# The causal mask moves from TensorE's score products to VectorE's maximum pass, with new order tables for the attention stage

## The chip, the cores and the metric

The kernel runs on one core of a Trainium2 chip. The core has five engines with an instruction queue each: TensorE (PE, matrix products into the banks of PSUM), VectorE (DVE), ScalarE (ACT), GpSimd (POOL) and SyncE (SP, which issues most DMAs). Sixteen DMA engines move data between HBM and SBUF. An engine runs its own queue in order; between engines only semaphores set the order. The metric is the device time of one execution, in microseconds (us).

## What the kernel computes

Two transformer-like layers on x, 4 sequences of 512 tokens, width 256, in fp32. Layer 0 is an attention pooling and a mixture of 32 experts. Layer 1 adds a conditioned product, and then runs causal attention with 16 heads of 16 and a mixture of 8 experts. Cut to the part that the change touches (the kernel treats 16 blocks of 256 tokens, called batches below, as its sequences; LB is 16 and T is 256 in it):

```python
h = layernorm(x, ln1_g, ln1_b)
q, k, v = split(h @ Wqkv)                    # 16 heads of 16
q, k = rope(q), rope(k)
scores = einsum('bqhd,bkhd->bhqk', q, k) / sqrt(16)
scores = where(tril, scores, -1e9)           # the causal mask
probs = softmax(scores)                      # exp(s - max s) / sum
x = x + (probs @ v) @ Wproj
h2 = layernorm(x, ln2_g, ln2_b)
top_inds = top_k(softmax(h2 @ Wgate), 2)     # two of 8 experts per token
...                                          # experts on gathered rows, added to x
```

## The kernel before

The program has three stages. Up to about 608 us layer 0 is computed. From there to about 1095 us the attention of layer 1 runs, and from 1139 us to the end its experts. All instructions that the change touches belong to the attention stage.

Attention works on 16 batches of 256 tokens. The 16 heads of a batch are taken in four groups of four. For one group the scores fill three banks of PSUM, called parts: part 0 and part 1 hold the later 128 queries of two heads each against all 256 keys (128x512), part 2 holds the first 128 queries of all four heads against the first 128 keys (128x512). A part passes through these steps:

- scores (PE, L1337 to L1346): a product of the bf16 triangle `causal` with `ident_b` writes the mask into the bank, and the product of KS and QS is added to it. For parts 0 and 1 the mask product has 256 columns, for part 2 it has 512.
- row_max (DVE, L1553): one reduction gives the negated maxima of a part, 2 or 4 numbers per row, into `smax`.
- exp (ACT, L1459): one exponential for each head, from the bank to PN in SBUF, with the negated maximum as bias. There are two slots of PN (NPN is 2), and the bank is free when its exponentials are done (semaphore s_pn).
- turn_p (PE, L1365, then ACT, L1467): PN is transposed, and copied to PT.
- values (PE, L1378 and L1380): the products with the values of the group.

Around these steps stand those of a whole batch, which belong to neighbouring batches at any moment. "combine" (DVE, L1561) adds four gathered expert results of layer 0 to X; they are gathered by POOL's indirect DMAs "got" (L1292). "matrix" is the conditioned product (DVE writes XC, L1567). "norm 0" and "norm 1" are the statistics of the two layer norms (DVE, L1519 to L1524), after which POOL takes the power -1/2 (L1273, tile rs), and "scale 0" and "scale 1" apply them (DVE, L1528, tiles xn and XN; XN has two buffers). "qk" is the product with Wqkv (PE, L1412), whose two rotary products DVE writes (L1593, tile rm) and POOL adds (L1301 and L1302). "split" (ACT and DVE, L1597) cuts q and k into high and low parts, and "stack" (SP, L1268) moves these to QS and KS by 16 DMAs of 128 KB for a batch. "proj" writes the residual XR (DVE, L1613), "base" adds it to X (POOL, L1305) and SP sends X to `out` (L1241). "normed" (SP, L1244) sends XN to a table in HBM; the semaphores xn2_out release its buffer. "gate" gives the routing logits, copied by DVE (L1617). The routing of a pair of batches, "route" and "place", is DVE work on small tiles (L187 to L312), and "entry" writes it to a table by POOL's indirect DMAs (L1314), eight for each pair. So every second round holds a placement and its eight entries. Layer 0's results are gathered three batches ahead, so that the last rounds have no "got".

The order of all this is written out by hand. There is one table for each engine (PE_ROUND, DVE_ROUND, ACT_ROUND, POOL_ROUND, SP_ROUND, from L1138). `rounds(table)` goes through its table once for each i from -4 to 19, and emits a step with offset o for batch i+o if that batch exists. One pass is called a round here. A step that waits on an engine holds up all the later steps of that engine's table.

PE's light steps (all but scores, turn_p and values) take turns on two banks in the order of its table (`light_bank`), and each of them waits until the one before it on its bank has been copied (`light_free`).

Of the kernel before, what the change touches and what calls it, by code (L numbers as in the profile page):

```python
# [61 lines left out]
def shape_constants():  # L62
# [35 lines left out]
def _build(nc, ctx, io, out):  # L98
# [1016 lines left out]
    s_attn_in = sem("attn_weights_in")  # L1115
    s_got0, s_ws_in = sems("results0_in", NGA * TB), sems("matrix_in", 2)
    s_begun = sem("values_begun_masks_ready")
# [21 lines left out]
        ("rank", -3), ("scores", -1, 3, 0), ("turn_p", -1, 2, 2), ("scores", -1, 3, 1), ("values", -1, 1),  # L1139
        ("norm_turn", 1), ("turn_p", -1, 2, 0), ("turn_p", -1, 2, 1), ("gate_turn", -2), ("scores", -1, 3, 2),  # L1140
        ("qk", 1, 0), ("qk", 1, 1), ("values", -1, 2), ("turn_p", -1, 3, 2), ("gate", -2), ("turn_p", -1, 3, 0),
        ("turn_p", -1, 3, 1), ("scores", 0, 0, 0), ("scores", 0, 0, 1), ("scores", 0, 0, 2), ("turn_qk", 1, 0),
        ("values", -1, 3), ("v", 1), ("outputs", -1, 0), ("scores", 0, 1, 0), ("turn_p", 0, 0, 2),
        ("outputs", -1, 1), ("scores", 0, 1, 1), ("turn_qk", 1, 1), ("scores", 0, 1, 2), ("turn_p", 0, 0, 0),
        ("out_turn", -1), ("turn_p", 0, 0, 1), ("scores", 0, 2, 0), ("x_turn", 2), ("proj", -1),
        ("scores", 0, 2, 1), ("matrix", 2), ("turn_p", 0, 1, 2), ("scores", 0, 2, 2), ("turn_p", 0, 1, 0),
        ("values", 0, 0), ("turn_p", 0, 1, 1))
# [299 lines left out]
    def act_attn(e):  # L1447
        wait_experts0(e)
        e.wait_ge(s_attn_in, N_ATTN_IN)
        for step, b, d in rounds(ACT_ROUND):  # L1450
            if step == "exp":
# [463 lines left out]
```

## Time and profile before

| what | us |
|---|---|
| median of three runs | 1525.74 |
| lowest and highest of them | 1524.75, 1528.5 |
| the profiled execution | 1527.01 |
| its span, first to last instruction | 1525.2 |
| busy: PE, DVE, ACT, POOL | 1392.3, 1033.8, 906.0, 721.4 |

The profiled execution lies 1.27 us above the median, and its span 1.81 us below its own time. The shares of busy time are means over three stages with different limits, so that the attention stage is read by itself: by stretches of one round each, by the timelines of its engines, and by the groups of instructions in it. In a timeline row the first number is the start in us, the second the duration, and a bracket at the end tells how long the engine had been idle and what released it. Durations of neighbouring instructions overlap in the pipeline, so the pace of a chain is read from one start to the next.

### The profile page before, as it was taken

How to read it: one execution, taken by the hardware profiler on the slowest of the kernel's cores; microseconds unless marked ns; L12 is line 12 of the kernel's file. 1: busy time of each engine (PE TensorE's matmuls, PEld its weight loads, DVE VectorE, ACT ScalarE, POOL GpSimd, SP SyncE). 2: the span in 40 equal slices, each digit the busy share in tenths (PEclk: the TensorE clock that was granted, in tenths of full speed). 3: DMA queues.
4: the chain of work that ended last, by engine and by line, in shares of the span. 5: the costliest groups of instructions: out<-in, count | busy, mean ns of one | idle time of the engine just before them, and what ended most of it. 6: DMA issues, size and time to landing. Idle time of an engine off the chain costs nothing.

```text
span 1525.2 us, 27526 instructions
## 1 busy us (share of the span) xinstructions
PE 1392.3 (91%) x9776; PEld 1221.8 (80%) x9776; DVE 1033.8 (68%) x2435; ACT 906.0 (59%) x2156; POOL 721.4 (47%) x720
## 2 busy tenths in 40 slices
PE   7997699999999999589999999999519999999996
PEld 5876599999999998358778777777419999998996
DVE  2999477777777775567888988895526556556552
ACT  5886255555555543158888888888526546456452
POOL 0788653444344204435465665653252435445333
PEclk9998899999999999689999999999859999999999
DMA  5421256566666614287868678686351343234212
GB/s 171 146 78 37 62 161 181 170 186 180 177 178 186 181 53 123 53 138 139 170 119 165 151 142 172 130 134 104 111 141 21 90 104 95 58 79 100 39 22 28
DMA packets 139449, 182.00 MB, mean 119 GB/s; under 512 B 22486, under 2 KB 107297, under 8 KB 139313
## 3 DMA queue, kind: packets, MB, share of 16 engines
q1 hardware_dynamic: 111152, 128.28, 33.6%
q0 software_dynamic: 28160, 51.96, 16.8%
q8 instruction: 79, 1.29, 0.4%
q14 instruction: 58, 0.47, 0.1%
HBM read 107.28 MB, written 42.08 MB: 98 GB/s over the span
## 4 chain that ended last, share of the span: by engine, by line
PE 78%; DVE 9%; issue 5%; POOL 3%; DMA 2%; ACT 2%; SPq 1%; POOLq 0%; DVEq 0%; ACTq 0%
PE banks L921 50%; PE banks L1365 5%; PE banks L1322 5%; PE banks L1412 3%; PE banks L440 3%; PE banks L983 2%; PE banks L1378 2%; PE banks L1339 2%; DVE lane_at L504 1%; PE banks L1759 1%; PE banks L1426 1%; DVE X L1561 1%; POOL table L1314 1%; PE banks L1346 1%; PE banks L1337 1%
## 5 line engine op out<-in xcount | busy, mean ns | idle before, releaser
L921 PE MATMUL banks<-hi_x,hi_w 128*128 128x320 f32 (+1 forms) x832 | 286.8, 345 | 10.7 <-DVE hidden L956 5.1
L921 PE MATMUL banks<-lo_x,hi_w 128*128 128x320 f32 (+1 forms) x832 | 285.6, 343 | 0.0
L921 PE MATMUL banks<-hi_x,lo_w 128*128 128x320 f32 (+1 forms) x832 | 285.2, 343 | 0.0
L921 PE MATMUL banks<-hi_w,hi_h 128*128 128x256 f32 x896 | 260.2, 290 | 2.1 <-DVE X L1010 1.7
L921 PE MATMUL banks<-lo_w,hi_h 128*128 128x256 f32 x896 | 253.5, 283 | 0.0
L921 PE MATMUL banks<-hi_w,lo_h 128*128 128x256 f32 x896 | 253.5, 283 | 0.0
L863 POOL DMA_INDIRECT xe<-pooled,idx x160 | 156.3, 977 | 198.6 <-PE banks L983 149.2
L1746 POOL DMA_INDIRECT out<-X,tab x64 | 106.5, 1664 | 204.7 <-DVE X L1843 190.1
L1459 ACT ACTIVATE PN<-banks,smax 128x256 f32<-128x256 f32 (+1 forms) x512 | 180.3, 443 | 15.9 <-DVE smax L1553 15.9
L921 PEld LDWEIGHTS banks<-hi_x,hi_w 128*128 128x128 f32 x832 | 158.3, 190 | 24.3 <-issue 10.4
L921 PEld LDWEIGHTS banks<-hi_w,hi_h 128*128 128x128 f32 x896 | 171.2, 191 | 3.3 <-issue 1.3
L921 PEld LDWEIGHTS banks<-lo_w,hi_h 128*128 128x128 f32 x896 | 171.5, 191 | 0.3
L921 PEld LDWEIGHTS banks<-hi_w,lo_h 128*128 128x128 f32 x896 | 171.3, 191 | 0.0
L921 PEld LDWEIGHTS banks<-hi_x,lo_w 128*128 128x128 f32 x832 | 158.0, 190 | 13.2
L921 PEld LDWEIGHTS banks<-lo_x,hi_w 128*128 128x128 f32 x832 | 158.3, 190 | 12.0
L1292 POOL DMA_INDIRECT got<-done,slot x128 | 124.5, 973 | 89.4 <-DMA done<-res 56.4
L1804 ACT ACTIVATE hidden<-banks,b1s 128x512 f32<-128x512 f32 x128 | 87.8, 686 | 122.8 <-PE banks L921 122.8
L1832 DVE TENSOR_TENSOR lo_h<-hidden,hi_h 128x512 fp32r<-128x512 f32 x128 | 88.3, 691 | 76.4 <-ACT hi_h L1809 76.4
L1553 DVE TENSOR_REDUCE smax<-banks 128x2 f32<-128x512 f32 (+1 forms) x192 | 126.8, 681 | 10.5 <-PE banks L1339 8.9
L956 DVE TENSOR_TENSOR hidden<-gate,banks 128x320 f32<-128x320 f32 (+1 forms) x144 | 73.4, 510 | 83.3 <-PE banks L921 74.9
L947 ACT ACTIVATE gate<-banks 128x320 f32<-128x320 f32 (+1 forms) x144 | 65.5, 455 | 97.6 <-PE banks L921 97.5
L1467 ACT ACTIVATE PT<-banks 128x512 f32<-128x512 f32 x192 | 114.5, 615 | 14.3 <-PE banks L1365 13.4
(186 smaller groups left out, 3051.4 us busy)
## 6 DMA issues: line engine op xcount, KB each, us to landing
w<-in_L_ffn_w SPq DMA_DIRECT2D x96, 256.0 KB, 5.8
done<-res SPq DMA_DIRECT2D x32, 640.0 KB, 3.9
QS<-parts_qk SPq DMA_DIRECT2D x128, 128.0 KB
KS<-parts_qk SPq DMA_DIRECT2D x128, 128.0 KB, 8.1
BIG<-in_L_ffn_W SPq DMA_DIRECT2D x16, 1024.0 KB, 9.6
mask<-in_c_masks SPq DMA_DIRECT2D x16, 257.0 KB, 2.8
pooled<-XF SPq DMA_DIRECT2D x16, 256.0 KB, 3.2
WS<-in_L_cond_W SPq DMA_DIRECT2D x16, 256.0 KB, 5.7
```

The costliest lines, as they stand in the source:

```text
L863: e.indirect_dma_start(xe[:, n % NXE, i, :], None, pooled, bass.IndirectOffsetOnAxis(ap=idx0[:, n * NS0 + i:n * NS0 + i + 1], axis=0)).the ...
L921: last = e.matmul(o, a[i], b[j], start=start and k == 0, stop=stop and k == 2, skip_group_check=True)
L956: e.tensor_tensor(hidden[:, i, 0:w], gate[:, i, 0:w], PS[:, up_bank(pt, unit) + 1, 0:w], ALU.mult).then_inc(s_hidden, 1)
L1292: e.indirect_dma_start(got0[:, b % NGA, t, k, :], None, done0, bass.IndirectOffsetOnAxis(ap=slot0[:, TB * b + t, k:k + 1], axis=0)).then_i ...
L1322: last = e.matmul(PS[:, bank, t * D:(t + 1) * D], src[:, c, t * P:(t + 1) * P], w(c), start=(c == 0), stop=(c == DC - 1))
L1365: last = e.transpose(PS[:, bank, k * P:(k + 1) * P], src, ident[:, :])
L1459: e.activation(PN[:, slot, part, x * width:(x + 1) * width], PS[:, part, x * width:(x + 1) * width], ACT.Exp, bias=smax[:, slot, col + x:c ...
L1467: e.activation(PT[:, G % NPN, part, :], PS[:, TBANK + n % 2, :], ACT.Copy).then_inc(s_pt, 1)
L1553: e.tensor_reduce(smax[:, G % NPN, col:col + heads_], PS[:, part, :].rearrange("p (x k) -> p x k", x=heads_), AX.X, ALU.max, negate=True). ...
L1746: e.indirect_dma_start(out_rows, bass.IndirectOffsetOnAxis(ap=who(u, i), axis=0), res1[:, u % 3, i, :], None, bounds_check=N - 1, oob_is_e ...
L1804: e.activation(hidden1[:, m % NHF, :], PS[:, 2 + m % 3, :], ACT.Gelu, bias=b1s[:, n, d:d + 1]).then_inc(s_hidden1, 1)
L1832: e.tensor_tensor(lo_h1[:, d, :], hidden1[:, m % NHF, :], hi_h1[:, d, :].bitcast(F32), ALU.subtract).then_inc(s_h1_lo, 1)
```

## The change

The mask products on PE are gone, with the tiles `causal` and `ident_b` and the two casts that made them. A tile `masks` (128 zeros, then the triangle) is loaded. The maximum pass becomes one fused instruction for each head: it adds the mask to the scores in the bank, writes the negated sum to PN, and gives its minimum, which is the negated maximum. The exponential then works in place in PN, with scale -1, and waits for each head. A bank of scores is now free when DVE has passed it (s_smax), and the wait for a free slot of PN is DVE's instead of ACT's. The small copy of the routing logits ("gate") moves from DVE to ACT. Two loads share another semaphore in the last stage.

```diff
-    tri_q = np.where(p[None, :] > p[:, None], -1e9, 0.0)
+    tri_q = np.concatenate([np.zeros((P, P)), np.where(p[None, :] > p[:, None], -1e9, 0.0)], 1)
...
 def pe_scores(e, G, part):
         if G >= 1:
-            e.wait_ge(s_pn, exp_count(G - 1, part))
-        if part < 2:
-            pair = 2 * g + part
-            e.matmul(PS[:, part, :].rearrange("p (h a k) -> p h a k", h=HQ, a=2)[:, :, 1, :], ident_b[:, :],
-                     wide(causal[:, :], 1, [P, HQ, P]), start=True, stop=False, skip_group_check=True)
...
+            e.wait_ge(s_smax, exp_count(G - 1, part))
+        for x in range(1 if part < 2 else 2):
+            pair = 2 * g + (part if part < 2 else x)
+            o, q, k = ((PS[:, part, :], QS[b % 2][:, pair, P:T], KS[b % 2][:, :, pair, :]) if part < 2 else
+                       (PS[:, 2, x * T:(x + 1) * T], QS[b % 2][:, pair, 0:P], KS[b % 2][:, :, pair, 0:P]))
+            last = e.matmul(o, q, k, start=True, stop=True, skip_group_check=True)
...
 def act_attn(e):
-                e.wait_ge(s_smax, 3 * G + part + 1)
-                if G >= NPN and part == 0:
-                    e.wait_ge(s_pt_ps, 3 * (G - NPN + 1))
                 for x in range(heads_):
-                    e.activation(PN[:, slot, part, x * width:(x + 1) * width], PS[:, part, x * width:(x + 1) * width], ACT.Exp,
-                                 bias=smax[:, slot, col + x:col + x + 1]).then_inc(s_pn, 1)
+                    s = PN[:, slot, part, x * width:(x + 1) * width]
+                    e.wait_ge(s_smax, 8 * G + col + x + 1)
+                    e.activation(s, s, ACT.Exp, bias=smax[:, slot, col + x:col + x + 1], scale=-1.0).then_inc(s_pn, 1)
...
 def dve_attn(e):
                 if G >= NPN and part == 0:
-                    e.wait_ge(s_pn, 8 * (G - NPN + 1))
-                e.tensor_reduce(smax[:, G % NPN, col:col + heads_], PS[:, part, :].rearrange("p (x k) -> p x k", x=heads_),
-                                AX.X, ALU.max, negate=True).then_inc(s_smax, 1)
+                    e.wait_ge(s_pt_ps, 3 * (G - NPN + 1))
+                for x in range(heads_):
+                    cols = slice(x * width, (x + 1) * width)
+                    e.tensor_tensor_reduce(PN[:, slot, part, cols], PS[:, part, cols], masks[:, T - width:], -1.0, 3.0e38,
+                                           ALU.add, ALU.min, smax[:, slot, col + x:col + x + 1]).then_inc(s_smax, 1)
...
     SP_ROUND = (
-        ("base", -3), ("weights", 2), ("stack", 1, 0), ("stack", 1, 1), ("normed", -2))
+        ("normed", -3), ("weights", 3), ("stack", 2, 0), ("stack", 2, 1), ("base", -1))
```

All five tables are new. Three places show what they move.

The first is DVE, where a pair of batches gets its slots (`slot`, step "place"), before the change: the placement stands behind the two scalings (XN and xn) and ahead of both sums of gathered results (X) and the rotary products (rm).

```order
L1528 TENSOR_SCALAR xn<-XC,mv,rs 128x256 [waits xn_turned,inverse_deviation0]
L1528 TENSOR_SCALAR xn<-XC,mv,rs 128x256
L294 TENSOR_TENSOR sm<-banks,small 128x32 [waits route1_ranked]
L295 TENSOR_REDUCE add<-sel 128x8
L297 SCALAR_TENSOR_TENSOR sm<-banks,sm 128x32 [waits dve_steps]
L299 TENSOR_TENSOR cum<-cum,add 128x8 [waits dve_steps]
L304 TENSOR_TENSOR pick<-hit,sm 128x64 [waits route1_placed]
L310 TENSOR_REDUCE sf<-pick 128x8 [waits route1_picked]
L312 TENSOR_SCALAR slot<-sf 128x8 [waits dve_steps]
L1561 SCALAR_TENSOR_TENSOR X<-got,w_pick,X 128x256 [waits results0_in2]
L1561 SCALAR_TENSOR_TENSOR X<-got,w_pick,X 128x256 [waits results0_added] x3
L1553 TENSOR_REDUCE smax<-banks 128x2 [waits exponentials,scores_part0]
```

After the change the same placement stands at the end, behind the second sum and ahead of the maxima of the next batch's first group (the fused pass is called ISA here).

```order
L1552 SCALAR_TENSOR_TENSOR X<-got,w_pick,X 128x256 [waits results0_in3]
L1552 SCALAR_TENSOR_TENSOR X<-got,w_pick,X 128x256 [waits results0_added] x3
L294 TENSOR_TENSOR sm<-banks,small 128x32 [waits route1_ranked]
L295 TENSOR_REDUCE add<-sel 128x8
L297 SCALAR_TENSOR_TENSOR sm<-banks,sm 128x32 [waits dve_steps]
L299 TENSOR_TENSOR cum<-cum,add 128x8 [waits dve_steps]
L304 TENSOR_TENSOR pick<-hit,sm 128x64 [waits route1_placed]
L310 TENSOR_REDUCE sf<-pick 128x8 [waits route1_picked]
L312 TENSOR_SCALAR slot<-sf 128x8 [waits dve_steps]
L1544 ISA PN,smax<-banks,masks 128x256 [waits weights1_turned,scores_part0]
```

Moved is "place": from a point behind "scale 0" to the last point ahead of the next batch's maxima.

The second is POOL in a round with entries, before: the four entries (`table`) that stand ahead of these rows go first, then the rotary sums (rm), and then the rest mixed with the gathers (got), the residual sum and the two powers (rs).

```order
L1302 TENSOR_TENSOR rm<-rm 128x8x32
L1301 TENSOR_TENSOR rm<-rm 128x8x32 [waits rotary_products]
L1302 TENSOR_TENSOR rm<-rm 128x8x32
L1314 DMA table<-pair,slot 8192x2 x2
L1292 DMA got<-done,slot 128x256 [waits results0_added]
L1292 DMA got<-done,slot 128x256 x3
L1314 DMA table<-pair,slot 8192x2 x2
L1292 DMA got<-done,slot 128x256 x2
L1305 TENSOR_TENSOR X<-X,XR 128x512 [waits residual_ready]
L1273 TENSOR_TENSOR rs<-ve,nhalf 128x2 [waits variance1]
L1292 DMA got<-done,slot 128x256
L1273 TENSOR_TENSOR rs<-ve,nhalf 128x2 [waits variance0]
```

After: rotary sums and residual sum come ahead, and all eight entries with six gathers stand between them and the power for "scale 0" (variance0).

```order
L1303 TENSOR_TENSOR X<-X,XR 128x512 [waits residual_ready]
L1312 DMA table<-pair,slot 8192x2 [waits route1_weighted,route1_slots]
L1312 DMA table<-pair,slot 8192x2
L1290 DMA got<-done,slot 128x256
L1312 DMA table<-pair,slot 8192x2 x2
L1290 DMA got<-done,slot 128x256
L1312 DMA table<-pair,slot 8192x2 x2
L1290 DMA got<-done,slot 128x256 x2
L1312 DMA table<-pair,slot 8192x2 x2
L1290 DMA got<-done,slot 128x256 x2
L1271 TENSOR_TENSOR rs<-ve,nhalf 128x2 [waits variance0]
L1290 DMA got<-done,slot 128x256 [waits results0_added]
```

The gathers and entries behind the rotary sums are now one block of 14, with the power at its end.

The third is SP's queue, around the stacking of one batch, before: the table transfer (normed) follows at once.

```order
L1268 DMA QS<-parts_qk 16x4x512 [waits scores_part2,qk_lo]
L1268 DMA QS<-parts_qk 16x4x512 x7
L1268 DMA KS<-parts_qk 16x4x512 [waits qk_lo]
L1268 DMA KS<-parts_qk 16x4x512 x7
L1244 DMA normed<-XN 128x2x256 [waits xn2_ready]
L1241 DMA out<-X 128x2x256 [waits base_ready]
L1251 TENSOR_LOAD in_itok_B_30_ptr [waits conditioned]
L1251 REGISTER_ALU
L1251 TENSOR_LOAD in_itok_B_30
L1251 ISA x2
```

After: the transfer of X to `out` follows first, and then "normed", whose batch is by one round older than before beside the same stack (offset -3 at the head of a round, behind a stack of offset 2 in the round ahead; it was -2 behind a stack of offset 1).

```order
L1266 DMA QS<-parts_qk 16x4x512 [waits scores_part2,qk_lo]
L1266 DMA QS<-parts_qk 16x4x512 x7
L1266 DMA KS<-parts_qk 16x4x512 [waits qk_lo]
L1266 DMA KS<-parts_qk 16x4x512 x7
L1239 DMA out<-X 128x2x256 [waits base_ready]
L1242 DMA normed<-XN 128x2x256 [waits xn2_ready]
L1249 TENSOR_LOAD in_itok_B_30_ptr [waits conditioned]
L1249 REGISTER_ALU
L1249 TENSOR_LOAD in_itok_B_30
L1249 ISA x2
```

Counted in batches, "normed" of batch b is now issued behind the stack of batch b+4; it stood behind the stack of batch b+3.

## Rows read from the trace of the kernel before

**Rows 1.** Windows, rounds: PE, PEld, DVE, ACT, POOL busy (x), clock, DMA share, GB/s.
```profile
714.54:741.22 26.68, 26.68 (x214) 20.96 (x213) 21.57 (x49) 22.73 (x64) 13.73 (x16) 1.00 0.80 154
767.90:795.00 27.10, 27.10 (x219) 21.33 (x220) 22.89 (x54) 22.02 (x59) 17.44 (x20) 1.00 0.79 150
795.00:822.37 27.37, 26.55 (x213) 20.63 (x211) 24.66 (x66) 23.70 (x65) 17.67 (x19) 1.00 0.74 154
960.00:987.33 27.33, 26.53 (x213) 20.60 (x211) 23.94 (x65) 23.65 (x65) 17.64 (x19) 1.00 0.85 155
1041.72:1070.31 28.59, 26.55 (x223) 22.06 (x223) 17.83 (x50) 25.79 (x75) 9.89 (x10) 0.94 0.71 112
```

**Rows 2.** Timeline, PE (start, us, engine, line, operation): mask product, score, transposes.
```profile
797.89 0.27 PE L1337 MATMUL banks<-causal,ident_b 128*128 128x256 bf16 x1
...
798.24 0.60 PE L1365 MATMUL banks<-ident,PN 128*128 128x128 f32 x4
...
799.89 0.38 PE L1342 MATMUL banks<-causal,ident_b 128*128 128x512 bf16 x1
...
800.34 0.60 PE L1365 MATMUL banks<-ident,PN 128*128 128x128 f32 x4
```

**Rows 3.** Timeline, DVE: three maxima in a row; the top-8 choice; layer norm; rotary products.
```profile
794.45 1.87 DVE L1553 TENSOR_REDUCE smax<-banks 128x2 f32<-128x512 f32 x3
...
796.94 0.77 DVE L234 MAX8 tv<-ex 128x8 f32<-128x8 f32 x4
...
801.93 0.08 DVE L238 MATCH_VALUE_LOAD ti<-tv,ex 128x8 f32 x1
...
803.66 0.68 DVE L1553 TENSOR_REDUCE smax<-banks 128x2 f32<-128x512 f32 x1
...
807.43 0.75 DVE L1519 BATCH_NORM_STATS2 st<-XC 128x6 f32<-128x256 f32 x2
...
808.57 0.69 DVE L1553 TENSOR_REDUCE smax<-banks 128x4 f32<-128x512 f32 x1
...
815.15 1.29 DVE L1593 TENSOR_TENSOR rm<-banks,ropec 128x512 f32<-128x512 f32 x2 [1.45 <-PE banks L1412]
```

**Rows 4.** Timeline, DVE: the fused mask and maximum in layer 0's pooling.
```profile
40.61 0.42 DVE L695 CUSTOM_DVE_ANT_0 pr<-banks,mask 128x256 f32<-128x256 f32 x1 [0.44 <-PE banks L585]
...
40.96 0.42 DVE L695 CUSTOM_DVE_ANT_0 pr<-banks,mask 128x256 f32<-128x256 f32 x1
```

**Rows 5.** Timeline, POOL, the same stretch.
```profile
40.32 0.72 POOL L272 TENSOR_TENSOR two<-hit 128x256 f32<-128x256 f32 x1 [39.35 <-DVE hit L246]
```

**Rows 6.** Lines by form, ACT: exponential from PSUM, exponential from SBUF.
```profile
L1459 ACT ACTIVATE PN<-banks,smax 128x256 f32<-128x256 f32 x225 | 93.8, 493 | 0.1
L643 ACT ACTIVATE pr<-pr,nmax 128x256 f32<-128x256 f32 x32 | 16.0, 503 | 3.9 <-DVE nmax L695 3.8
```

**Rows 7.** Timeline, POOL: scatters and gathers of attention.
```profile
785.94 1.00 POOL L1314 DMA_INDIRECT table<-pair,slot  x1 [0.30 <-issue]
...
796.35 0.97 POOL L1292 DMA_INDIRECT got<-done,slot  x1 [0.30 <-issue]
...
806.87 0.72 POOL L1273 TENSOR_TENSOR rs<-ve,nhalf 128x2 f32<-128x2 f32 x1 [0.56 <-DVE ve L1524]
...
839.07 1.01 POOL L1314 DMA_INDIRECT table<-pair,slot  x1 [1.61 <-DVE slot L312]
```

**Rows 8.** Timeline, DVE: slots of a pair, and sums of gathered results.
```profile
838.10 0.17 DVE L312 TENSOR_SCALAR slot<-sf 128x8 uint32<-128x8 f32 x1
838.18 2.04 DVE L1561 SCALAR_TENSOR_TENSOR X<-got,w_pick,X 128x256 f32<-128x256 f32 x4
...
844.95 3.72 DVE L1561 SCALAR_TENSOR_TENSOR X<-got,w_pick,X 128x256 f32<-128x256 f32 x4
```

**Rows 9.** Timeline, SP: stacking of one batch and what follows it.
```profile
797.05 5.19 SPq L1268 DMA_DIRECT2D QS<-parts_qk  x8
...
807.87 0.59 SPq L1244 DMA_DIRECT2D normed<-XN  x1
808.51 0.51 SPq L1241 DMA_DIRECT2D out<-X  x1
```

**Rows 10.** Tile XN: its transfer to the table in HBM.
```profile
DMA to landing us min/median/max: 2.2/8.7/12.2
```

**Rows 11.** Timeline, PE, end of attention: the longest wait of its transposes.
```profile
1059.39 0.66 PE L1365 MATMUL banks<-ident,PN 128*128 128x128 f32 x4 [1.41 <-ACT PN L1459]
```

More of the change, by code:

```diff
@@ L1138, in _build @@
     PE_ROUND = (
[L1139 to L1147, printed above, removed]
-    DVE_ROUND = (
-        ("route", -3, 3), ("row_max", -1, 2, 0), ("proj", -2), ("row_max", -1, 2, 1), ("norm", -2, 1),
-        ("matrix", 1), ("norm", 1, 0), ("row_max", -1, 2, 2), ("scale", -2, 1), ("scale", 1, 0), ("place", -3),
-        ("combine", 2, 0), ("row_max", -1, 3, 0), ("row_max", -1, 3, 1), ("qk", 1, 0), ("row_max", -1, 3, 2),
-        ("qk", 1, 1), ("combine", 2, 1), ("gate", -2), ("route_shift", -2), ("row_max", 0, 0, 0),
-        ("row_max", 0, 0, 1), ("row_max", 0, 0, 2), ("split", 1, 0), ("route", -2, 1), ("outputs", -1, 0),
-        ("row_max", 0, 1, 0), ("outputs", -1, 1), ("row_max", 0, 1, 1), ("split", 1, 1), ("row_max", 0, 1, 2),
-        ("route", -2, 2))
@@ new lines, in _build @@
+        ("scores", 0, 1, 2), ("out_turn", -1), ("turn_p", 0, 0, 0), ("scores", 0, 2, 0), ("turn_p", 0, 0, 1),
+        ("scores", 0, 2, 1), ("x_turn", 2), ("proj", -1), ("scores", 0, 2, 2), ("matrix", 2),
+        ("turn_p", 0, 1, 2), ("scores", 0, 3, 0), ("turn_p", 0, 1, 0))
+    DVE_ROUND = (
+        ("route_shift", -3), ("outputs", -2, 0), ("outputs", -2, 1), ("row_max", -1, 1, 0),
+        ("row_max", -1, 1, 1), ("split", 0, 1), ("row_max", -1, 1, 2), ("route", -3, 1), ("route", -3, 2),
+        ("row_max", -1, 2, 0), ("proj", -2), ("row_max", -1, 2, 1), ("row_max", -1, 2, 2), ("matrix", 1),
+        ("norm", 1, 0), ("row_max", -1, 3, 0), ("row_max", -1, 3, 1), ("scale", 1, 0), ("norm", -2, 1),
+        ("route", -3, 3), ("combine", 2, 0), ("row_max", -1, 3, 2), ("qk", 1, 0), ("scale", -2, 1), ("qk", 1, 1),
+        ("combine", 2, 1), ("place", -3), ("row_max", 0, 0, 0), ("row_max", 0, 0, 1), ("split", 1, 0),
+        ("row_max", 0, 0, 2))
@@ L1327, in pe_scores @@
         b, g = divmod(G, NG)
-        if G == 0 and part == 0:
-            e.wait_ge(s_begun, 4)
         if part == 0 and g == 0:
@@ L1511, in act_attn @@
                                  bias=lng[:, 3, c:c + 1], scale=lng[:, 2, c:c + 1]).then_inc(s_h2T, 1)
+            elif step == "gate":
+                half = (b % GB) * TB * E1
+                e.wait_ge(s_lg1, b + 1)
+                e.activation(lgs[:, half:half + TB * E1], PS[:, light_bank["gate", b, d], 0:TB * E1], ACT.Copy).then_inc(s_lgs, 1)
             elif step == "route_exp" and pair_begins(b):
```

67 lines of the change are left out of this document (28 added, 39 removed).

## Prediction

> **What bounds the kernel now.** I read the attention stage by itself, first the windows of one round each. In a round without placements PE is busy for all of its 26.68 us, while DVE has 21.57, ACT 22.73 and POOL 13.73 [rows 1]. The eight rounds from 767.90 to 987.33 hold placements, entries and gathers; a pair of them takes (987.33 - 767.90) / 4 = 54.86 us. There PE is still busy for 26.5 to 27.1 of about 27.4 us, DVE for 22.9 to 24.7, and POOL's load has risen to 17.5. The reader is to see that PE is the bound and that DVE is the next one, 3 to 4 us behind it. Second, the timelines: how long each instruction keeps its engine is the distance to the next start, as the printed durations overlap. Third, the queues that DVE depends on (POOL and SP), since a new order can make these late although they are not busy for the whole round.
>
> **PE.** A mask product and its score take 798.24 - 797.89 = 0.35 us for 256 + 512 columns, and for part 2, with 512 + 512 columns, 800.34 - 799.89 = 0.45 [rows 2]. By columns the mask is 0.11 of the first and 0.22 of the second. A batch has 8 of the first and 4 of the second: 8 x 0.11 + 4 x 0.22 = 1.76 us. PE's round falls from 26.68 to 24.9, and over 16 batches 28 us is the most that the change can give.
>
> **DVE.** Twelve reductions go; three in a row take 1.87 of which the last is 0.68, so that one costs 0.60 [rows 3]: 7.2 us per batch. In come 32 fused passes, 16 of 128x256 and 16 of 128x128. The wide one runs in layer 0, at 40.96 - 40.61 = 0.35 (its accumulator read included) [rows 4]. The narrow one is in no row. It costs no less than half of the wide one, 0.17, and no more than the wide one, 0.35. From 0.60 for 512 columns and 0.35 for 256, 128 columns come to 0.22, and I take this. So 16 x 0.345 + 16 x 0.22 = 9.0 (bounds 8.2 and 11.1), which is 1.8 more than before. The gate copy takes 0.1 off every round. DVE's pair of rounds, 22.89 + 24.66 = 47.55, becomes 51.0, which is 25.5 a round: DVE overtakes PE. In the rounds without routing it has 21.57 + 1.8 = 23.4, under PE.
>
> The Trainium skill ("VectorE: DVE Perf Modes", section on the TRN2 errata) charges a VectorE instruction reading PSUM 120 cycles and one per column at 0.96 GHz. That would be 0.39 us for 256 columns and 0.26 for 128, an estimate of 10.4 us per batch instead of 9.0. It speaks against cutting one wide pass into heads; the pace of 0.35 in the trace is below its 0.39 [rows 4], so that I stay with the rows. By the page the sum below would hardly move, because the waits below absorb slower passes, but the first rival would lose most of its gain.
>
> **ACT.** The exponentials read SBUF instead of PSUM: 503 ns in layer 0 against 493 [rows 6], 0.3 for 32; the gate copy adds 0.2. From 22.0 to 23.7 ACT rises to at most 24.2, still behind DVE and PE. This costs nothing as long as these are later.
>
> **Wait 1, POOL.** The power for "scale 0" now stands behind a block of eight entries and six gathers, and the block can't start before "place", which has moved to the end of DVE's round. An entry costs 1.00 + 0.30 and a gather 0.97 + 0.30 [rows 7]: 8 x 1.30 + 6 x 1.27 = 18.0 us. The first entry starts 839.07 - 838.27 = 0.8 after the end of the slots [rows 7, 8]. With 0.72 for the power the scaling can go on 19.5 us after the slots. What DVE has to do between: 16 wide passes 5.5; 12 narrow ones 2.6; two splits, XR and XC, each at the 0.60 of a 512-wide pass, 2.4; two scalings of outputs 1.4 (an estimate from 0.35 a pass and as much for the reciprocal); the choice of experts, 0.77 for MAX8 and 803.66 - 801.93 = 1.73, 2.5; one norm 808.57 - 807.43 = 1.14 [rows 3]. The sum is 15.5. So DVE stands still for 4.0 us in each round after a placement (bounds 2.5 and 5). Behind "scale 0" on DVE are the sums, the rotary products and the maxima of the last group; PE's qk and then everything of the next batch waits for these. Before, POOL had the same entries, but "place" came a round's half earlier, and its powers were ready for DVE's statistics: the power at 806.87 waited for DVE [rows 7].
>
> **Wait 2, SP.** "normed" of a batch b-2 now goes out behind the stack of batch b+2 and one transfer to `out`, and "scale 1" of batch b must wait until it has landed, because XN has two buffers. From the start of QS to the issue of "normed" 807.87 - 797.05 = 10.8; the transfer to `out` ahead of it 808.51 - 807.87 = 0.64; its own issue 0.59; then the landing, median 8.7 [rows 9, 10]. That is 20.7 us after the first split. DVE's work from there to "scale 1": 12 wide passes 4.1, 16 narrow 3.5, split, XR and XC 1.8, two norms 2.3, outputs 1.4, "scale 0" 0.7, the first sum 2.0, rotary products 1.3, and some 0.7 of waiting for PE's qk (it is 1.45 before [rows 3], and more work lies ahead of it now): 17.8. The stall is 3.0, with the landings from 2.2 to 12.2 anything from none to 6. In the round with wait 1 it is hidden by that; so it is due once in a pair. Before, this transfer had a round more.
>
> **The sum.** A pair: 51.0 of work, 4.0 and 3.0 of the waits, twice 0.7 for qk: 59.4 against 54.86, which is +4.5, and for four such pairs +18. Three early rounds without routing and without a second use of XN run at PE's new pace, 3 x -1.8 = -5.4. The last three rounds have no gathers, so that the block of POOL is short; there PE and DVE share the limit and I take -1.3 each, -4. The clock: after an idle time of 1.41 us PE was granted a lower clock in the stage's end, 0.94 in the mean of that round [rows 1, 11]. In rounds with stalls PE has 4 us to spare, so that I take only +2 for all (bounds 0 and 14). Start and end of the stage I count as unchanged, within 1 us. Together +10.6: 1527.0 + 10.6 = 1537.6 for an execution like the profiled one, and less the 1.3 that this lies above the median, 1536. This case has its own range from 1524 (landings early, entries 1.2 us faster) to 1550.
>
> **Rivals.**
> 1. Neither wait decides, because DVE comes later to "scale 0" and "scale 1" than my sums say, or POOL's block runs faster. Then the eight rounds take DVE's 25.5 instead of 27.4, -15.4, and with the 9.4 of the other rounds the time is 1501. For it speaks that the pure work of every engine fits into 25.5 us, and that only 2 to 4 us of slack are missing; against it that POOL's pace is the same in each row. It decides if the slots are done 4 us earlier than I put them.
> 2. One of the waits decides, the other doesn't. With wait 1 alone a pair is 56.4 (+1.5), with wait 2 alone 55.4 (+0.5): 4 x +1 - 9.4 = -5, 1520. For it speaks that the landing varies from 2.2 to 12.2 [rows 10].
> 3. Each stall lowers PE's clock, and PE's products at 1.2 GHz then lie on the chain to DVE: some 1.5 us for each of eight stalls, 1550. Before, one idle time of 1.41 did this [rows 11]; against it, PE has scores to run in most of a stall.
> 4. DVE's fused passes are held up by POOL as the sums are: four of these took 2.04 us at 838.18 and 3.72 at 844.95 [rows 8], where POOL was adding. By that ratio, for the two thirds of a round that POOL works, the passes would take 9.0 x 0.55 = 4.9 us more in a round: about 1600. Against it, in layer 0 the pace was 0.35 while POOL was at a product of 0.72 from 40.32 on [rows 4, 5].
>
> On the last, the Trainium skill ("SBUF — State Buffer", section "Who interferes with whom") says that a VectorE instruction with two inputs in SBUF contends with a GpSimd instruction that reads SBUF, and one with at most one such input does not. The sums have two and the fused pass one, so it agrees with both rows; by the page's rule rival 4 would be out altogether.
>
> **Chances.** My forecast 0.54; rival 1 0.17; rival 2 0.14; rival 3 0.08; rival 4 0.04; something else 0.03. A measurement of this kernel can tell about 0.3%, 4.6 us, from no change. Slower by more comes from most of my own case (0.42 of 0.54) and rivals 3 and 4: 0.55. Faster by more from rival 1, half of rival 2 and a little of the rest: 0.27. Within it 0.18. The range from 1500 to 1556 takes in rivals 1 and 2 and most of 3.
>
> **What would show it.** In the changed profile PE should have no bf16 products of 256 or 512 columns, and rounds without routing should last about 25 us. A wait of DVE's xn on POOL's rs of about 4 us in every second round, and one of DVE's XN on the transfer "normed" of about 3 us in the other, would show the two waits; PE's busy time in these rounds would fall to some 25 of 29 us. The fused narrow pass at a pace of 0.22 would show DVE's term. I am wrong if xn and XN hardly wait, or if rounds from 770 us on last 26 us or less.

## The result, and the profile after

The changed kernel took 1571.83 us (median of 4 runs, 1568.62 to 1577.71), the kernel before 1526.82 on the same chip: a ratio of 1.030, 95% interval 1.026 to 1.034. It is slower, by 45 us; forecast were 1536 and a range from 1500 to 1556. The direction was right, and the time lies outside the range. The profiled execution of the changed kernel has a span of 1566.9 us, 41.7 more than before.

The windows of rounds of the changed kernel, in the columns of [rows 1], cut where xn starts:

```profile
703.20:730.00 26.80, 25.67 (x202) 19.78 (x201) 24.52 (x101) 23.49 (x59) 14.27 (x16) 1.00 0.79 132
730.00:757.30 27.30, 26.17 (x203) 20.05 (x202) 25.97 (x112) 24.71 (x68) 14.07 (x16) 1.00 0.79 155
757.30:784.00 26.70, 25.39 (x200) 19.44 (x200) 24.91 (x103) 23.17 (x58) 14.16 (x16) 1.00 0.71 148
784.00:817.70 33.70, 27.95 (x215) 21.16 (x213) 27.75 (x121) 26.52 (x71) 21.85 (x23) 1.00 0.73 141
817.70:845.40 27.70, 25.71 (x191) 19.17 (x192) 24.97 (x101) 21.52 (x54) 14.42 (x16) 0.94 0.63 115
784.00:1033.60 249.60, 217.97 (x1621) 166.35 (x1620) 208.53 (x881) 192.49 (x497) 144.46 (x152) 0.95 0.69 131
1064.10:1092.00 27.90, 26.91 (x222) 20.39 (x220) 20.01 (x103) 26.07 (x66) 6.88 (x8) 1.00 0.69 100
```

The kernel before, its eight rounds for the same batches, cut at xn too ([rows 1] has them cut at another point):

```profile
782.02:1001.45 219.43, 214.67 (x1718) 167.91 (x1717) 190.93 (x473) 183.14 (x490) 141.10 (x153) 1.00 0.77 149
```

Three things can be read. A round without a placement takes 26.7 to 27.3 us ahead of the eight, as before, although PE is busy for only 25.4 to 26.2 of it. The first round that has a placement, up to the next xn, takes 33.7; the three others take 35.3, 37.0 and 34.7. And the eight rounds with placements, entries and gathers take 249.60 us, 62.4 for a pair, where they took 219.43 and 54.86: these alone are 30.2 us of the 41.7. Of the rest, 2.0 us had been lost when they begin (784.0 against 782.0), and 9.5 us are lost behind them. PE's granted clock in the eight is 0.95 in the mean, where it was 1.00.

What VectorE waited for from 650 to 1140 us in the changed kernel (waiting instruction, what released it; us in total, times, longest):

```profile
DVE XN L1518 <- issue: 16.6, 5, 6.4
DVE xn L1518 <- POOL rs L1271: 15.0, 4, 4.5
DVE XR L1603 <- PE banks L1320: 13.8, 10, 5.8
DVE rm L1584 <- PE banks L1400: 13.1, 14, 2.0
```

The first two are the two waits of the prediction. "issue" behind XN means that the profile shows no releaser; the next rows tell what it was. The queue of SP in the round that leads to one such wait, changed kernel:

```profile
843.59 0.58 SPq L1239 DMA_DIRECT2D out<-X  x1
844.22 0.50 SPq L1242 DMA_DIRECT2D normed<-XN  x1
```

"normed" is issued at 844.22, and XN, which needs that buffer, starts 10.5 us after that, at 854.71. In the trace the transfer lands at 854.62, 0.09 us before XN starts. VectorE in the same pair of rounds:

```profile
854.71 0.74 DVE L1518 TENSOR_SCALAR XN<-XR,mv,rs 128x256 f32<-128x256 f32 x2 [2.60 <-issue]
...
856.56 3.63 DVE L1552 SCALAR_TENSOR_TENSOR X<-got,w_pick,X 128x256 f32<-128x256 f32 x4
...
861.06 0.17 DVE L312 TENSOR_SCALAR slot<-sf 128x8 uint32<-128x8 f32 x1
...
880.70 0.79 DVE L1518 TENSOR_SCALAR xn<-XC,mv,rs 128x256 f32<-128x256 f32 x2 [2.88 <-POOL rs L1271]
...
887.21 1.13 DVE L1518 TENSOR_SCALAR XN<-XR,mv,rs 128x256 f32<-128x256 f32 x2
```

XN has waited 2.60 us at 854.71, and xn 2.88 us at 880.70, for POOL. The latter's releaser, on POOL's timeline:

```profile
862.04 1.01 POOL L1312 DMA_INDIRECT table<-pair,slot  x1 [2.13 <-DVE slot L312]
863.35 1.00 POOL L1312 DMA_INDIRECT table<-pair,slot  x1 [0.30 <-issue]
864.65 0.99 POOL L1290 DMA_INDIRECT got<-done,slot  x1 [0.30 <-issue]
...
878.93 0.98 POOL L1290 DMA_INDIRECT got<-done,slot  x1 [0.30 <-issue]
879.92 0.75 POOL L1271 TENSOR_TENSOR rs<-ve,nhalf 128x2 f32<-128x2 f32 x1
```

The slots are done at 861.23, the first entry starts 0.8 later, as in [rows 7], and the power ends at 880.67, which is 19.4 us behind the slots. The prediction had 19.5.

Last, the end of the stage, where the prediction had seen no wait; one of XN on VectorE, again for a transfer "normed" that had been issued at 1088.12:

```profile
1096.69 0.74 DVE L1518 TENSOR_SCALAR XN<-XR,mv,rs 128x256 f32<-128x256 f32 x2 [6.44 <-issue]
```

### The profile page after: what moved, and what is told of

Same layout as the page of the kernel before. It is cut to its first block, busy times and chain, and to the rows that moved or that the text cites. A ratio compares the mean times of both kernels' runs of the same rounds, so it can differ in the third digit from the quotient of the medians.

```text
span 1566.9 us, 27911 instructions
## 1 busy us (share of the span) xinstructions
PE 1395.2 (89%) x9584; PEld 1217.6 (78%) x9584; DVE 1066.6 (68%) x3249; ACT 923.9 (59%) x2172; POOL 727.3 (46%) x720
## 4 chain that ended last, share of the span: by engine, by line
PE 61%; DVE 12%; issue 7%; SPq 7%; DMA 6%; POOL 5%; ACT 2%; POOLq 0%; DVEq 0%; ACTq 0%
PE banks L921 49%; SPq L1266 5%; DMA normed<-XN 4%; DVE X L1552 2%; PE banks L983 2%; POOL table L1312 2%; DVE rm L1584 2%; PE banks L1353 1%; PE banks L1400 1%; PE banks L440 1%; PE banks L1320 1%; DVE PN L1544 1%; POOL got L1290 1%; DVE XN L1518 1%; PE banks L1745 1%
## 5 line engine op out<-in xcount | busy, mean ns | idle before, releaser
L1446 ACT ACTIVATE PN<-PN,smax 128x256 f32<-128x256 f32 (+1 forms) x512 | 191.4, 452 | 4.2 <-DVE smax L1544 3.3
L1544 DVE CUSTOM_DVE_ANT_0 PN<-banks,masks 128x256 f32<-128x256 f32 (+1 forms) x512 | 150.6, 351 | 11.9 <-PE banks L1335 6.2
L1353 PE MATMUL banks<-ident,PN 128*128 128x128 f32 x768 | 120.4, 285 | 7.3 <-ACT PN L1446 4.1
L1453 ACT ACTIVATE PT<-banks 128x512 f32<-128x512 f32 x192 | 110.9, 594 | 26.8 <-PE banks L1353 25.8
```

What stands on the lines that cost most here:

```text
L1353: last = e.transpose(PS[:, bank, k * P:(k + 1) * P], src, ident[:, :])
L1446: e.activation(s, s, ACT.Exp, bias=smax[:, slot, col + x:col + x + 1], scale=-1.0).then_inc(s_pn, 1)
L1453: e.activation(PT[:, G % NPN, part, :], PS[:, TBANK + n % 2, :], ACT.Copy).then_inc(s_pt, 1)
L1544: e.tensor_tensor_reduce(PN[:, slot, part, cols], PS[:, part, cols], masks[:, T - width:], -1.0, 3.0e38, ALU.add, ALU.min, smax[:, slot, c ...
```

## The experiments

Every run was compared with runs of the kernel before on the same chip. The runs fell on four chips, and on two of them the kernel before took 1662 and 1678 us instead of 1527. There engines stood idle for stretches that no instruction of the program ended, as in this row of VectorE's waits with the old tables (run e4_old_tables):

```profile
DVE rsum L1590 <- remote: 57.6, 11, 8.3
```

What these stretches are stays open. Times are compared on one chip only, between chips the ratios.

**e1_normed_early.** SP's transfer one batch earlier.

```diff
     SP_ROUND = (
-        ("normed", -3), ("weights", 3), ("stack", 2, 0), ("stack", 2, 1), ("base", -1))
+        ("normed", -2), ("weights", 3), ("stack", 2, 0), ("stack", 2, 1), ("base", -1))
```

> SP's table has the transfer normed one batch earlier (offset -2), so that it stands behind the stack of batch b+3 again; nothing else differs from the changed kernel. Theory W (the two queue waits and VectorE's own work add up on VectorE's chain): the waits of XN (12 us in the four pairs of rounds) go, the waits of xn on POOL stay, and the time falls by 10 to 16 us, from 1572 to 1556 to 1562. Rival F (the waits only fill time that VectorE would lose anyway to TensorE): XN's waits go and others take their place, time 1567 to 1573.

Measured: 1704.73 us against 1661.96 of before, ratio 1.026 (1.020 to 1.032). No wait of XN for its transfer is left. The chip was one of the slower two, where the changed kernel itself was not run, and xn's waits on POOL were down to 1.7 us in all. So this run by itself decides nothing.

**e2_power_early.** POOL's power behind two gathers instead of six.

```diff
     POOL_ROUND = (
-        ("got", 3, 0, 0), ("norm", -2, 1), ("got", 3, 0, 1), ("qk", 1, 0), ("qk", 1, 1), ("base", -2),
-        ("entry", -3, 0), ("got", 3, 0, 2), ("entry", -3, 1), ("got", 3, 0, 3), ("entry", -3, 2),
-        ("got", 3, 1, 0), ("got", 3, 1, 1), ("entry", -3, 3), ("got", 3, 1, 2), ("got", 3, 1, 3), ("norm", 2, 0))
+        ("got", 3, 0, 0), ("got", 3, 0, 1), ("got", 3, 0, 2), ("norm", -2, 1), ("got", 3, 0, 3), ("qk", 1, 0),
+        ("qk", 1, 1), ("base", -2), ("entry", -3, 0), ("entry", -3, 1), ("got", 3, 1, 0), ("entry", -3, 2),
+        ("got", 3, 1, 1), ("entry", -3, 3), ("norm", 2, 0), ("got", 3, 1, 2), ("got", 3, 1, 3))
```

> POOL's table has the power for scale 0 behind eight entries and two gathers instead of behind eight entries and six; four gathers follow it. SP's table as in the changed kernel. Theory W: xn's waits on POOL (15 us in four rounds) go, but part of each is then taken by the wait of XN on the transfer normed, which starts from an earlier point and was hidden in that round: time down by 8 to 15 us, to 1557 to 1564. Rival F: 1567 to 1573.

Measured on the same chip: 1687.07 us, ratio 1.017 (1.010 to 1.023), 17.7 less than with the other edit alone. One wait of XN of 6.3 us was left.

**e3_both and e8_both_again.** Both edits; first beside e1 and e2, then beside the changed kernel on one chip, which is run **e7_after_again**.

> Both edits. Theory W: no wait of over 1 us of xn or XN is left, a pair of rounds falls from 62.4 to about 55.5, and the time by 24 to 32 us, to 1540 to 1548. It stays slower than the kernel before, since VectorE's own work (some 26.5 us in a round) has taken TensorE's place as the bound. Rival F: 1560 to 1573. Rival P (VectorE has slack, and without the waits TensorE's shorter round shows): a pair at 50 to 51, time 1520 or less.

Measured: 1682.08 us, ratio 1.012 (1.006 to 1.017). It is 22.7 below e1 and 5.0 below e2. In e1's profile xn waits for POOL for only 1.7 us, so on this chip that wait doesn't account for the 22.7; what does is open. The two waits are therefore judged by the next pair of runs, on a quicker chip.

> The changed kernel as it is, as the reference of the next three on one chip. Ratio to the kernel before 1.03 again, if the loss doesn't depend on the chip; on a chip where rounds are longer for other reasons the waits of xn and XN could be smaller, ratio down to 1.02.

> Both order edits (normed one batch earlier, power for scale 0 behind two gathers instead of six), beside the changed kernel on one chip. Theory W: 24 to 32 us less than the changed kernel. Rival F (the waits only fill time that is lost anyway): 0 to 8 us less.

Measured: the changed kernel 1576.09 (ratio 1.031, 1.029 to 1.033), both edits 1543.90 (ratio 1.011, 1.009 to 1.014). That is 32.2 us less, where theory W had 24 to 32 and rival F 0 to 8. The waits removed had been 16.6 + 15.0 = 31.6 us in the first profile of the changed kernel. In that of e7, on the chip of e8, they are longer:

```profile
DVE XN L1518 <- issue: 20.7, 6, 6.4
DVE xn L1518 <- POOL rs L1271: 16.2, 4, 4.5
```

These are 36.9 us, and the profiled executions of e7 and e8 differ by 37.1. So the two waits cost about what they last, and F falls. The absolute time expected for both edits, 1540 to 1548, holds on this chip.

**e4_old_tables and e10_old_tables_again.** The new mechanism with the five tables of the kernel before; the logits copy is VectorE's again, since these tables have it there.

```diff
     SP_ROUND = (
-        ("normed", -3), ("weights", 3), ("stack", 2, 0), ("stack", 2, 1), ("base", -1))
+        ("base", -3), ("weights", 2), ("stack", 1, 0), ("stack", 1, 1), ("normed", -2))
...
```

> The mask on VectorE and the exponentials in place, with all five order tables of the kernel before and the logits copy on VectorE. Theory W (the new order causes the two waits, the mechanism only makes VectorE the bound): no waits of over 1 us on rs and normed, rounds of 26.5 to 27.5, time 1520 to 1535, about that of the kernel before. Rival M (the fused passes themselves, more passes in line with the same other work, cost the time): 1550 or more. Rival P: TensorE's 1.8 us a round shows, 1500 to 1510.

> The mask on VectorE with all five order tables of the kernel before, again; the first time the chip was one on which the kernel before took 1662 us. If the order makes the whole loss: ratio to the kernel before 0.99 to 1.005. If that first equality came from the chip's longer rounds, which hid a loss of VectorE's: 1.01 to 1.02.

Measured: 1661.60, ratio 1.000 (0.997 to 1.003), and on the quicker chip 1530.40, ratio 1.002 (1.000 to 1.004). So the mechanism alone, with 1.7 us more of VectorE in each of the eight rounds (204.62 us against 190.93) and its shorter TensorE, changes the time by no more than 0.4%, and the loss of the changed kernel comes with the new order. Rivals M and P both fall. The new tables were not run with the old mechanism, so it stays open whether they would cost as much without the move of the mask. The windows of e10 (two rounds without entries, then the eight with):

```profile
702.10:728.60 26.50, 25.03 (x196) 19.32 (x196) 23.46 (x100) 22.97 (x57) 13.47 (x16) 1.00 0.78 131
728.60:756.20 27.60, 25.93 (x212) 19.62 (x204) 25.30 (x118) 24.80 (x69) 13.61 (x16) 1.00 0.85 154
782.30:1005.30 223.00, 205.51 (x1628) 156.71 (x1624) 204.62 (x890) 190.00 (x489) 139.47 (x153) 1.00 0.76 148
```

PE is busy for 25.0 to 25.9 us in the first two, and for 205.51 of 223.00 in the eight; what PE saves it now spends waiting. PE's largest waits in the eight rounds:

```profile
PE banks L440 <- DVE xn L1514: 6.4, 8, 1.7
PE banks L1414 <- DVE parts_qk L1584: 5.9, 8, 1.1
```

**e5_base_later.** Both edits, and POOL's residual sum behind one gather.

```diff
-        ("got", 3, 0, 0), ("got", 3, 0, 1), ("got", 3, 0, 2), ("norm", -2, 1), ("got", 3, 0, 3), ("qk", 1, 0),
-        ("qk", 1, 1), ("base", -2), ("entry", -3, 0), ("entry", -3, 1), ("got", 3, 1, 0), ("entry", -3, 2),
+        ("got", 3, 0, 0), ("got", 3, 0, 1), ("got", 3, 0, 2), ("norm", -2, 1), ("qk", 1, 0), ("qk", 1, 1),
+        ("got", 3, 0, 3), ("base", -2), ("entry", -3, 0), ("entry", -3, 1), ("got", 3, 1, 0), ("entry", -3, 2),
```

> As the kernel with both edits, and POOL's residual sum (base) comes one gather later, so that it no longer runs beside the second sum of gathered results on VectorE. Theory W with VectorE as the bound: the second sum falls from 3.65 to about 2.7 us, and the time by 0.9 x 14 = 10 to 14 us against both edits. If VectorE isn't the bound: within 3 us of it.

Measured: 1546.59, against 1543.90 with both edits: nothing gained, a miss of theory W's 10 to 14. The sums became shorter by 7% only (625 ns each instead of 674), and their waits for gathered results longer (4.9 us instead of 2.7).

**e6_half_sums.** Both edits, with two of the four sums cut to 8 columns.

```diff
-                    e.scalar_tensor_tensor(X[:, tt, :], got0[:, b % NGA, d[0], k, :], w_pick0[:, tt, k:k + 1], X[:, tt, :],
+                    n = D if k < 2 else 8
+                    e.scalar_tensor_tensor(X[:, tt, 0:n], got0[:, b % NGA, d[0], k, 0:n], w_pick0[:, tt, k:k + 1], X[:, tt, 0:n],
                                            ALU.mult, ALU.add).then_inc(s_comb, 1)
```

> As the kernel with both edits, with a part of layer 1's input left out: of the four gathered results per token the third and fourth are added in 8 of 256 columns only, which takes about 2.4 us of VectorE's work out of each round. Theory W with VectorE as the bound: rounds without waits fall from 26.8 to TensorE's 25.5 to 26, the time by 15 to 30 us against both edits. If TensorE or a chain through all engines is the bound already: 0 to 6 us.

Measured: 1529.62, 14.3 less than both edits, just under theory W's 15 to 30. Less work was taken away than meant. The groups of the sums from 690 to 1040 (line, engine, operation, form, count; busy us, mean ns), first e8, then e6:

```profile
L1552 DVE SCALAR_TENSOR_TENSOR X<-got,w_pick,X 128x256 f32<-128x256 f32 x96 | 64.7, 674 | 5.2 <-DMA got<-done,slot 2.7
```

```profile
L1553 DVE SCALAR_TENSOR_TENSOR X<-got,w_pick,X 128x256 f32<-128x256 f32 x48 | 28.4, 592 | 6.6 <-DMA got<-done,slot 5.8
L1553 DVE SCALAR_TENSOR_TENSOR X<-got,w_pick,X 128x8 f32<-128x8 f32 x48 | 22.4, 468 | 1.7
```

64.7 us became 28.4 + 22.4 = 50.8, 13.9 us less. In the whole stage 81.5 became 36.8 + 26.9 = 63.7, 17.8 less, and the time fell by 14.3. So with the two waits gone most of VectorE's work counts. That it counts everywhere isn't shown: from the fourth xn to the last the two profiled executions differ by only 7.2 us (341.93 and 334.68), with 13.9 less of sums.

**e9_split_first.** In the profile of e8 one more wait shows, PE's, from 690 to 1040:

```profile
PE banks L1414 <- DVE parts_qk L1588: 17.2, 12, 2.0
```

This is the turning of the outputs (L1414). It uses the bank that holds q and k until VectorE has made the low part (parts_qk, step "split"). In e8's round at 854 that stood behind the second sum, the placement and four fused passes, first VectorE's rows, then PE's:

```profile
847.73 3.63 DVE L1552 SCALAR_TENSOR_TENSOR X<-got,w_pick,X 128x256 f32<-128x256 f32 x4
...
852.23 0.17 DVE L312 TENSOR_SCALAR slot<-sf 128x8 uint32<-128x8 f32 x1
...
854.09 0.69 DVE L1588 TENSOR_TENSOR parts_qk<-banks,parts_qk 128x512 fp32r<-128x512 f32 x1
```

```profile
854.83 0.66 PE L1414 MATMUL banks<-ident,oT 128*128 128x128 f32 x4 [2.03 <-DVE parts_qk L1588]
```

```diff
-        ("row_max", 0, 0, 0), ("row_max", 0, 0, 1), ("split", 1, 0),
+        ("split", 1, 0), ("row_max", 0, 0, 0), ("row_max", 0, 0, 1),
         ("row_max", 0, 0, 2))
```

> As the kernel with both order edits, and on VectorE the split of q's parts (split 1,0) stands ahead of the next batch's maxima of parts 0 and 1 instead of behind them. Theory S (a third wait: TensorE's turning of the outputs stands behind the shared bank that this split releases, 17 us in 12 waits from 690 to 1040, and it lies on the chain): the waits fall to under 0.6 us each and the time by 8 to 17 us against both edits, ratio to the kernel before 1.000 to 1.006. Rival D (VectorE's own work is the bound and the wait of TensorE costs nothing): 0 to 4 us, ratio 1.009 to 1.012.

Measured: 1537.53 against 1526.46 of before on its chip, ratio 1.006 (1.004 to 1.008). Over the kernel before it is 11.1 us where both edits had 16.6. The gain of 5.5 us by the medians, 8 by the ratios, is at or below the lower edge of theory S, and the ratio is outside what rival D had. What is left of the waits from 690 to 1040, on PE and on VectorE:

```profile
PE banks L1414 <- DVE parts_qk L1588: 5.2, 9, 1.1
```

```profile
DVE X L1552 <- DMA got<-done,slot: 8.5, 4, 3.4
```

The longest is 1.1 us, where under 0.6 was expected. The wait for gathers was 2.7 us in e8. It comes from the edit of POOL's table: the gathers stand behind the power, and arrive too late for the second sum.

**e12_no_new_waits and e13_old_tables_tuned.** e12 goes on from e9, with a new table for POOL and one step moved on VectorE:

```diff
     POOL_ROUND = (
+        ("got", 3, 0, 0), ("norm", -2, 1), ("got", 3, 0, 1), ("got", 3, 0, 2), ("qk", 1, 0), ("qk", 1, 1), ("base", -2),
+        ("got", 3, 0, 3), ("entry", -3, 0), ("got", 3, 1, 0), ("entry", -3, 1), ("got", 3, 1, 1), ("entry", -3, 2),
+        ("got", 3, 1, 2), ("got", 3, 1, 3), ("norm", 2, 0), ("entry", -3, 3))
...
-        ("row_max", -1, 3, 2), ("qk", 1, 0), ("scale", -2, 1), ("qk", 1, 1)
+        ("scale", -2, 1), ("row_max", -1, 3, 2), ("qk", 1, 0), ("qk", 1, 1)
```

e13 goes on from e10, with two exchanges on VectorE and one on POOL:

```diff
-        ("row_max", 0, 0, 2), ("split", 1, 0)
+        ("split", 1, 0), ("row_max", 0, 0, 2)
-        ("scale", -2, 1), ("scale", 1, 0)
+        ("scale", 1, 0), ("scale", -2, 1)
-        ("norm", -1, 1), ("got", 3, 1, 2), ("norm", 2, 0))
+        ("norm", -1, 1), ("norm", 2, 0), ("got", 3, 1, 2))
```

> As the kernel with both order edits and the split first, with POOL's table drawn up again: all gathers of a round stand ahead of the power for scale 0 and the last two entries behind it (with the gathers behind it, the second sum on VectorE waited 8.5 us for them in four rounds), and XN is scaled ahead of the rotary products, where POOL adds nothing (0.65 instead of 1.2 to 1.3 us). If what is left of the loss is the order's: the waits for gathers go, 6 to 14 us less than with the split first, ratio to the kernel before 0.997 to 1.002. If it is the mechanism's own work on VectorE: 0 to 4 us less, ratio 1.003 to 1.006.

> The mask on VectorE with the tables of the kernel before, and three exchanges in them: the split of q's parts ahead of the maxima of part 2, scale 0 ahead of scale 1, POOL's power for scale 0 ahead of a gather. TensorE waited 0.7 us for the split and 0.8 us for xn in each of eight rounds with the old tables. If these waits are on the chain, 8 to 16 us less than the old tables alone, ratio to the kernel before 0.992 to 0.997, faster than both kernels. If other engines' work follows at once: 0 to 4 us less, ratio 1.000 to 1.003.

Measured, on the slowest of the chips: e12 1679.53, ratio 1.002 (0.999 to 1.004), the kernel before 1677.58. In the profile of e12 VectorE's wait for gathers is gone. From 1.031 the new tables have come to 1.002 by order alone, with the mechanism untouched. The interval of e12 also takes in the lower part of what was expected if the mechanism's own work were left (1.003 to 1.006), so a small rest of that kind isn't excluded. e13 1683.95, ratio 1.004 (1.002 to 1.007), outside both of its expectations: its exchanges gained nothing, and no version beat the kernel before. Whether e12 or e13 would gain on a chip without the idle stretches wasn't tried.

## Why the prediction was wrong in size

**The two waits: right.** Each had its place, its releaser and about its size. POOL's was forecast at 4 x 4.0 us and came to 15.0 in four. SP's was forecast at 4 x 3.0: in the eight rounds it came three times, with 9.0 in all, a fourth time just behind them with 1.2, and with 6.4 more in the last rounds. Undoing both took 32 us away. PE's lower clock in these rounds came too; what it cost was not measured apart from the waits.

**The step that failed first: "Three early rounds ... run at PE's new pace, 3 x -1.8 = -5.4".** They gained nothing: from xn to xn the three take 80.83 us, where they took 80.02. PE's new pace was not what set them.
- PE's saving. PE's busy time fell from 26.68 to 25.7 (mean of the three rounds above), by 0.9, and with the old tables (e10) by 1.1 in the mean of the eight rounds (214.67 and 205.51, divided by 8). Forecast were 1.76. The price of one mask product was right where products follow each other without a wait. Four transposes and a wide score, with the mask, in the kernel before:

```profile
798.67 0.60 PE L1426 MATMUL banks<-ident,oT 128*128 128x128 f32 x4
799.11 0.27 PE L1337 MATMUL banks<-causal,ident_b 128*128 128x256 bf16 x1
799.14 0.48 PE L1339 MATMUL banks<-KS,QS 128*128 128x512 f32 x1
799.46 0.60 PE L440 MATMUL banks<-ident,rm 128*128 128x128 f32 x4
```

These take 799.46 - 798.67 = 0.79 us, and without the mask 745.91 - 745.24 = 0.67 (rows of the changed kernel below): 0.12 less, where the prediction had 0.11. Where the rest of the 1.76 went is open.
- DVE's work. The prediction took the lightest window, 21.57, for all early rounds. Every second round there has the choice of experts too, so that the mean of the three is 22.4 (67.13 / 3), and in the changed kernel it is 25.1 (75.43 / 3). Of the 8.3 us that this is more in three rounds, counted from each start to the next, the fused passes in place of the reductions make 4.4, the sums 2.8 and XN 1.3. So the passes cost 1.5 more in a round, where 1.8 was forecast; sums and XN, put at no change, cost another 1.3. With the pauses under 0.2 us between its instructions, 2.2 in all, DVE fills 77.6 of the 80.8 us, which leaves no room for the 24.9 us of PE's new pace. With the old tables (e10) DVE fills 73.9 of 80.2 us, and the three rounds are no shorter; what holds them there is open. The paces of the fused passes are 0.35 and 0.21, as forecast (first two rows 128x256, then 128x128):

```profile
728.60 0.42 DVE L1544 CUSTOM_DVE_ANT_0 PN<-banks,masks 128x256 f32<-128x256 f32 x1
...
728.95 0.42 DVE L1544 CUSTOM_DVE_ANT_0 PN<-banks,masks 128x256 f32<-128x256 f32 x1
...
733.87 0.28 DVE L1544 CUSTOM_DVE_ANT_0 PN<-banks,masks 128x128 f32<-128x128 f32 x1
...
734.08 0.28 DVE L1544 CUSTOM_DVE_ANT_0 PN<-banks,masks 128x128 f32<-128x128 f32 x1
```

The estimates of 0.39 and 0.26 from the Trainium skill ("VectorE: DVE Perf Modes", section on the TRN2 errata) are too long as paces by these rows.
- A wait that was missed. PE's outputs stand behind VectorE's split, through a shared bank. The changed kernel, PE in an early round:

```profile
742.62 0.96 PE L1429 MATMUL banks<-wgate,h2T 128*128 128x8 f32 x8
744.51 0.66 PE L1414 MATMUL banks<-ident,oT 128*128 128x128 f32 x4 [0.93 <-DVE parts_qk L1588]
744.92 0.48 PE L1335 MATMUL banks<-KS,QS 128*128 128x512 f32 x1
745.24 0.60 PE L1414 MATMUL banks<-ident,oT 128*128 128x128 f32 x4
745.59 0.48 PE L1335 MATMUL banks<-KS,QS 128*128 128x512 f32 x1
745.91 0.60 PE L1353 MATMUL banks<-ident,PN 128*128 128x128 f32 x4
```

PE is idle for 0.93 us at 744.51, and by the split of e8 for up to 2.03. The prediction wrote that in rounds with stalls "PE has 4 us to spare"; it asked what stands behind xn and XN, but not which of PE's steps stands behind a bank that VectorE has yet to leave. By the gain of e9 this wait lay on the chain in part of the stage. It did not hold up the early rounds: in e9 PE doesn't wait there for the split, and the three take 81.23 us.

**The second: the work of a pair, 51.0.** With the old tables (e10) it is right: 204.62 / 4 = 51.2. With the new ones DVE was busy for 208.53 / 4 = 52.1 us of a pair. To that come pauses between instructions that depend on each other, which the busy time of a window leaves out: 1.6 us of a pair, summed from those under 0.2 us. A sum of DVE's that is set against a round has to hold them. The waits came to 8.7 us of a pair, where 8.4 was forecast. The 1.1 us more of work lie in the sums and in XN, which now run beside POOL's adds. The first sum of a round takes 2.04 us, as before. The second takes 3.62 to 3.66 us in every round from 700 to 1044, where it took 2.4 to 2.7 and 3.6 to 3.8 in turn; the 3.72 of [rows 8] is one of the long ones. XN's scaling is told at the end. So what rival 4 had for the fused passes, that POOL holds them up, held for the sums and the scaling instead. By the ratios of e8, e9 and e12 most of the rest of the loss was order as well.

**The third: "The last three rounds have no gathers ... -4".** They gained nothing, and from the end of the eight rounds to the end of the program 9.5 us were lost. The wait of XN at 1096.69 took 6.44 us of it: without gathers and entries, VectorE comes to XN sooner, but "normed" is issued no sooner. The prediction looked for SP's wait only where POOL's was.

In sum: the eight rounds cost 30.2 us instead of 18, and the rounds ahead of them and behind them, forecast at -9.4, cost 2.0 and 9.5. The range was too narrow because its upper end had the waits at their longest, but every gain at its full size.

**Rivals.** 1 and 2 (a wait that doesn't decide) fell. 3 (PE's clock) can't be told apart from the waits. In the eight rounds PE was busy for 12.5 us longer than with the old tables at a clock of 1.00 (217.97 and 205.51), for nearly as many products; how much of that lay on the chain is open. With both edits (e8) the mean clock of these rounds is still 0.96. 4 fell: in e10, 75 of the fused passes overlap one of POOL's adds, and take 418 and 284 ns like the rest. That the mechanism alone would come to 1.002 was forecast by none of the prediction's cases: even with no new wait it gains nothing.

## What to carry to other kernels

When work moves from the engine that is the bound to the one behind it, the gain ends where that one becomes the bound: add up its work from start to start, pauses included, before counting the first engine's saving. A new order is priced queue by queue: for each wait, take the time from its releaser's start back to what that one waits for, and set it against the work of the engine that waits; this gave the mean of both waits over the four pairs to within 1 us (3.8 and 2.3 for 4.0 and 3.0), though not each one. Do the same for buffers and banks that two steps share, as these carry waits that no data shows.

## What the runs showed of the hardware that was not expected

A scaling pass on VectorE (TENSOR_SCALAR, one tensor from SBUF, 128x256) slows down when POOL adds in SBUF at the same time. In the changed kernel and with the old tables (e10), from 690 to 1040:

```profile
L1518 DVE TENSOR_SCALAR XN<-XR,mv,rs 128x256 f32<-128x256 f32 x22 | 11.9, 581 | 9.0 <-issue 9.0
```

```profile
L1514 DVE TENSOR_SCALAR XN<-XR,mv,rs 128x256 f32<-128x256 f32 x26 | 9.5, 408 | 0.0
```

In the first, XN stands between the two rotary products, whose sums POOL makes at that moment; in the second it stands ahead of them, and took 408 ns. Within the changed kernel the overlap decides: 21 of the 32 passes that write XN overlap one of POOL's adds and take 675 ns in the mean, the other 11 take 400 to 412. The same holds for the sums, which read two tensors from SBUF: 57 of 128 overlap an add and take 857 ns in the mean, the others 473 to 486. One of POOL's adds beside the pair of XN at 887.21 (1.13 us, above):

```profile
887.38 0.82 POOL L1299 TENSOR_TENSOR rm<-rm 128x256 f32<-128x256 f32 x1 [2.73 <-DVE rm L1584]
```

The Trainium skill ("SBUF — State Buffer", section "Who interferes with whom") counts tensor_scalar among the operations that can take the port pair shared with GpSimd, and the trace agrees, with 581 against 408 ns. The fused pass, with its one input in SBUF, kept its pace of 0.35 beside POOL's adds too.
